# Tridiagonalisation by Householder reflections: pivot and squared norm in a matmul of their own, reflector and update weights on other engines

## The reference, cut to what matters

```python
def _L0_gnn_ref(features, A, W1, b1, W2, b2):
    deg = jnp.sum(A, axis=0) + jnp.sum(A, axis=1) - jnp.diagonal(A)
    d_inv_sqrt = jnp.where(deg > 0, jax.lax.rsqrt(deg), 0.0)
    L_norm = d_inv_sqrt[:, None] * (jnp.diag(deg) - A) * d_inv_sqrt[None, :]
    _, U = jnp.linalg.eigh(L_norm)
    agg = jnp.einsum('mn,bnd->bmd', U.T, features)
    out = jax.nn.relu(agg @ W1 + b1) @ W2 + b2
    return jnp.einsum('nm,bmd->bnd', U, out)
```

## Time and profile before

| what | value |
|---|---|
| device time, median of 3 runs | 1482.2 us (1481.74 to 1482.93) |
| profiled execution: device time | 1483.62 us |
| profiled execution: span from first to last instruction | 1481.8 us |
| 127 reflections (L297 first to last) | 14.5 to 386.5 us |
| eigenvalues and vectors | about 390 to 665 us |
| layers | about 666 us to the end |
| mean granted TensorE clock | 0.888 of full speed |

### The profile page before, as it was taken

How to read it: one execution, slowest core, us unless ns; L and a number is a source line. 1 busy time by engine, 2 the same in 40 slices (tenths; PEclk the granted TensorE clock), 3 DMA queues, 4 the chain that set the end, 5 groups by cost and what they waited for, 6 DMA issues and landing times.

```text
span 1481.8 us, 24437 instructions
## 1 busy us (share of the span) xinstructions
PE 1024.0 (69%) x6001; PEld 834.4 (56%) x6001; DVE 1125.8 (76%) x5634; ACT 793.1 (54%) x2905; POOL 172.3 (12%) x464
## 2 busy tenths in 40 slices
PE   5777777777640000008998889988799978899875
PEld 4666666666430000005796666976668956679754
DVE  6888888888799889983457784566865678845677
ACT  3555555555320000004777866777767778677786
POOL 2111111111200000001011010111020120201111
PEclk9999999999975555558999899999899999999987
DMA  0000000000200000001000010000010000100000
GB/s 2 1 1 1 1 1 1 1 1 1 56 20 1 1 1 1 1 0 57 1 2 1 1 39 22 1 1 1 8 53 1 1 1 2 30 0 1 1 1 29
DMA packets 19903, 12.94 MB, mean 9 GB/s; under 512 B 1153, under 2 KB 18722, under 8 KB 19746
## 3 DMA queue, kind: packets, MB, share of 16 engines
q1 hardware_dynamic: 19746, 11.23, 2.8%
HBM read 7.03 MB, written 4.19 MB: 8 GB/s over the span
## 4 chain that ended last, share of the span: by engine, by line
PE 32%; DVE 11%; ACT 8%; issue 2%; POOL 1%; DMA 0%; DVEq 0%; POOLq 0%; ACTq 0%
PE P L1036 11%; PE P L981 6%; PE P L1044 6%; ACT x L1138 2%; PE P L986 2%; ACT S L1209 2%; DVE stats L1248 2%; PE P L1098 1%; DVE S L1320 1%; DVE top L1325 1%; DVE t L1338 1%; PE P L1053 1%; PE P L1082 1%; POOL t L969 1%; ACT t L1189 1%
## 5 line engine op out<-in xcount | busy, mean ns | idle before, releaser
L461 PE MATMUL sumP<-ident_tail,Yb 128*128 128x128 f32 x1 | 0.5, 473 | 215.6 <-DVE Yb L623 215.6
L193 PE MATMUL productP<-M,ident_tail 128*128 128x127 f32 (+63 forms) x254 | 87.3, 441 | 71.3 <-DVE M L313 71.3
L1036 PE MATMUL P<-t,WihT 128*128 128x128 f32 (+1 forms) x832 | 119.4, 290 | 10.9 <-POOL t L969 10.9
L1044 PE MATMUL P<-step_h,WhhT 128*128 128x128 f32 (+2 forms) x768 | 123.4, 304 | 0.0
L490 ACT ACTIVATE small<-small 128x1 f32<-128x1 f32 x1 | 0.2, 203 | 229.1 <-DVE small L596 229.1
L461 PEld LDWEIGHTS sumP<-ident_tail,Yb 128*128 128x128 f32 x1 | 0.2, 183 | 215.7 <-DVE Yb L623 215.7
L1036 PEld LDWEIGHTS P<-t,WihT 128*128 128x128 f32 x832 | 109.9, 191 | 14.4 <-POOL t L969 13.7
L193 PEld LDWEIGHTS productP<-M,ident_tail 128*128 128x128 f32 x254 | 63.6, 311 | 95.1 <-DVE M L313 95.1
L1161 ACT ACTIVATE gate_i<-P,half_bias 128x128 f32<-128x128 f32 (+3 forms) x160 | 69.1, 432 | 89.3 <-PE P L1044 65.3
L962 POOL TENSOR_TENSOR rstd<-variance,minus_half 128x4 f32<-128x4 f32 x64 | 64.5, 1007 | 442.4 <-DVE variance L1258 442.4
L1044 PEld LDWEIGHTS P<-step_h,WhhT 128*128 128x128 f32 x768 | 108.9, 191 | 4.5 <-DVE step_h L1291 0.7
(11 more groups left out here) (322 smaller groups left out, 3159.6 us busy)
## 6 DMA issues: line engine op xcount, KB each, us to landing
xin<-x SPq DMA_DIRECT2D x16, 256.0 KB, 2.8
out<-y SPq DMA_DIRECT2D x16, 256.0 KB, 2.3
W<-L_gnn_W SPq DMA_DIRECT2D x3, 64.0 KB
Wqkv<-L_gnn_W SPq DMA_DIRECT2D x1, 192.0 KB
Wg<-L_gnn_Wg SPq DMA_DIRECT2D x2, 64.0 KB
A<-adj SPq DMA_DIRECT2D x1, 64.0 KB, 2.0
b<-L_gnn_b SPq DMA_DIRECT2D x1, 64.0 KB
bg<-L_gnn_bg SPq DMA_DIRECT2D x1, 64.0 KB
```

Of the source, the lines that this page charges most:

```text
L193: pe.matmul(productP[:, remaining], tails, M[:, remaining], start=True, stop=True).then_inc(product_ready, 1)
L1036: last = pe.matmul(place, c["WihT"][:, p - 1, gate * H:(gate + 1) * H], sources(s, p, t), start=bank not in fresh, stop=not t, skip_group_ ...
L1044: last = pe.matmul(gate_place(s, p, t, gate), c["WhhT"][:, p - 1, gate * H:(gate + 1) * H], step_h[s][:, 0:G * windows(p)], start=False, s ...
```

## The change

The row product is split in two. TensorE first makes two columns alone, the pivot and the squared norm (into the new PSUM tile `pivotP`), then the row. ScalarE copies the two columns, takes the root, and copies the row when it comes; VectorE takes pivot and squared norm from the two-column copy. `v_col` is made on ScalarE and written straight into `reflectors`; beta goes straight into `E` and the gain straight into `gains`, with their signs turned once at the end of the loop (`E` on VectorE, `gains` on GpSimd in the next block). The weights of the second half of the update are put together from products that ScalarE (`SPREAD_V`, `GAINED_M`, `INNER_V`, `REST`) and GpSimd (`INNER`) make; of them VectorE keeps `SPREAD`, `PART` and `NU`. Per reflection VectorE has 15 arithmetic instructions in place of 17, ScalarE 10 in place of 8, GpSimd 3 in place of 2, TensorE 5 matmuls in place of 4.

```diff
@@ GpSimd, each reflection @@
                 pool.wait_ge(inverses_ready, now)
                 pool.sem_inc(inverses_seen, 1)
+                pool.wait_ge(beta_ready, now)
+                nc.gpsimd.tensor_tensor(col(INNER), inverses[:, 0:1], E[:, k:k + 1], ALU.mult).then_inc(inner_ready, 1)
                 nc.gpsimd.tensor_tensor(open_gain[:], inverses[:, 1:2], below[:, now:now + 1],
@@ TensorE @@
-                pe.matmul(tailP[:, now:N + 1], tails, ident_tail[:, now:N + 1], start=True, stop=True).then_inc(tail_row_ready, 1)
+                pe.matmul(pivotP[:, 0:2], tails, ident_tail[:, now:N + 1:N - now], start=True, stop=True).then_inc(pivot_ready, 1)
+                pe.matmul(tailP[:, remaining], tails, ident[:, remaining], start=True, stop=True).then_inc(tail_row_ready, 1)
@@ ScalarE @@
-                act.wait_ge(tail_row_ready, now)
-                nc.scalar.activation(row_square[parity][:, now:N + 1], tailP[:, now:N + 1], ACT.Copy).then_inc(row_copied, 1)
-                nc.scalar.activation(norm, tailP[:, N:N + 1], ACT.Sqrt, bias=tiny[:]).then_inc(norm_ready, 1)
+                act.wait_ge(pivot_ready, now)
+                nc.scalar.activation(pivots[parity][:], pivotP[:, 0:2], ACT.Copy).then_inc(pivot_copied, 1)
+                nc.scalar.activation(norm, pivotP[:, 1:2], ACT.Sqrt, bias=tiny[:]).then_inc(norm_ready, 1)
+                act.wait_ge(tail_row_ready, now)
+                nc.scalar.activation(rows[parity][:, remaining], tailP[:, remaining], ACT.Copy).then_inc(row_copied, 1)
                 act.wait_ge(beta_ready, now)
+                nc.scalar.activation(v_col, ident[:, now:now + 1], ACT.Identity, bias=tail, scale=beta).then_inc(v_ready, 1)
                 act.wait_ge(matrix_ready, now)
...
+                nc.scalar.activation(col(BETA_M), M[:, now:now + 1], ACT.Copy, scale=beta).then_inc(beta_m_ready, 1)
                 act.wait_ge(v_ready, now)
                 act.wait_ge(gain_ready, now)
...
+                nc.scalar.activation(col(NGV), v_col, ACT.Copy, scale=gain).then_inc(scaled_ready, 1)
+                act.wait_ge(spread_ready, now)
+                nc.scalar.activation(col(SPREAD_V), v_col, ACT.Copy, scale=col(SPREAD)).then_inc(spread_v_ready, 1)
+                act.wait_ge(beta_m_ready, now)
+                nc.scalar.activation(col(GAINED_M), col(BETA_M), ACT.Copy, scale=gain).then_inc(gained_m_ready, 1)
+                act.wait_ge(spread_v_ready, now)
+                act.wait_ge(inner_ready, now)
+                nc.scalar.activation(col(INNER_V), col(SPREAD_V), ACT.Copy, scale=col(INNER)).then_inc(inner_v_ready, 1)
+                act.wait_ge(gained_m_ready, now)
+                act.wait_ge(coef_ready, now)
+                nc.scalar.activation(col(REST), col(SPREAD_V), ACT.Identity, bias=col(GAINED_M),
+                                     scale=col(COEF)).then_inc(rest_ready, 1)
@@ VectorE @@
+                v.wait_ge(pivot_copied, now)
...
...
+                v.wait_ge(inverses_ready, now)
+                V.scalar_tensor_tensor(gain, inverses[:, 0:1], -1.0, norm, ALU.mult, ALU.mult).then_inc(gain_ready, 1)
+                V.tensor_tensor(col(SPREAD), inverses[:, 0:1], square, ALU.mult).then_inc(spread_ready, 1)
+                v.wait_ge(row_copied, now)
+                v.wait_ge(beta_ready, now)
+                whole_row = t.done(V.tensor_tensor(first, first, beta, ALU.add))
...
...
+                v.wait_ge(rest_ready, now)
+                part = t.done(V.scalar_tensor_tensor(col(PART), product_colP[:, 0:1], gain, col(REST), ALU.mult, ALU.add))
...
-                t.step(V.scalar_tensor_tensor(col(NU), col(NGV_NORM), col(G), col(NGP), ALU.mult, ALU.add))
+                v.wait_ge(inner_v_ready, now)
+                t.until(part)
+                t.step(V.scalar_tensor_tensor(col(NU), p_rowP[:, now:now + 1], col(INNER_V), col(PART), ALU.mult, ALU.add))
...
@@ VectorE, once, behind the loop @@
...
+            V.tensor_tensor(scrap[:], M[:], ident, ALU.mult).then_inc(diag_ready, 1)
...
@@ GpSimd, once, at the start of spectral_vectors @@
-            nc.gpsimd.tensor_tensor(T[:], ident, gains[:], ALU.mult).then_inc(gains_turned, 1)
+            t.step(nc.gpsimd.tensor_tensor(T[:], ident, gains[:], ALU.mult))
+            nc.gpsimd.tensor_scalar(T[:], T[:], -1.0, None, ALU.mult).then_inc(gains_turned, 1)
```

More of the change, by code:

```diff
@@ L62, in spectral_basis @@
     small = sb("small", [N, 32])
-    row_square = [sb(f"row_square_{j}", [N, N + 1]) for j in range(2)]
-    v_col = sb("v_col", [N, 1])
+    rows = [sb(f"row_{j}", [N, N]) for j in range(2)]
+    pivots = [sb(f"pivot_square_{j}", [N, 2]) for j in range(2)]
     tiny = sb("tiny", [N, 1])
@@ L115, in col @@
         return small[:, j:j + n]
-    (ABS, BETA, NTAU, NKB, COEF, Q, G, BETA_M, NGV, NGV_NORM, NGP, NU, DEGREE, DEG, DI, SOME, EXPONENT, DIAG, ROWSUM,
-     TABLE) = range(20)
+    (ABS, SPREAD, INNER, COEF, Q, BETA_M, GAINED_M, NGV, SPREAD_V, INNER_V, REST, PART, NU, DEGREE, DEG, DI, SOME, EXPONENT,
+     DIAG, ROWSUM, TABLE) = range(21)
     def every_reflection(reflect):
@@ L218, in reflect @@
                 act.wait_ge(beta_ready, now)
+                beta, v_col, gain = E[:, k:k + 1], reflectors[:, k:k + 1], gains[:, k:k + 1]
+                nc.scalar.activation(v_col, ident[:, now:now + 1], ACT.Identity, bias=tail, scale=beta).then_inc(v_ready, 1)
                 act.wait_ge(matrix_ready, now)
-                nc.scalar.activation(col(BETA_M), M[:, now:now + 1], ACT.Copy, scale=col(BETA)).then_inc(beta_m_ready, 1)
-                nc.scalar.activation(E[:, k:k + 1], col(BETA), ACT.Copy, scale=-1.0).then_inc(edges_ready, 1)
+                nc.scalar.activation(col(BETA_M), M[:, now:now + 1], ACT.Copy, scale=beta).then_inc(beta_m_ready, 1)
@@ L265, in reflect @@
                 after = k + 2
[L266 to L271, removed]
+                pivot, square = pivots[parity][:, 0:1], pivots[parity][:, 1:2]
+                first, v_row = rows[parity][:, now:now + 1], rows[parity][:, remaining]
+                sign, beta, gain = signs[:, k:k + 1], E[:, k:k + 1], gains[:, k:k + 1]
                 norm = divisors[parity][:, 1:2]
-                t.done(V.scalar_tensor_tensor(col(ABS), first, -1.0, first, ALU.mult, ALU.max))
-                prepared = t.done(V.tensor_scalar(sign, first, 0.0, 2.0, ALU.is_ge, ALU.mult))
+                v.wait_ge(pivot_copied, now)
+                t.done(V.scalar_tensor_tensor(col(ABS), pivot, -1.0, pivot, ALU.mult, ALU.max))
+                prepared = t.done(V.tensor_scalar(sign, pivot, 0.0, 2.0, ALU.is_ge, ALU.mult))
                 v.wait_ge(norm_ready, now)
@@ L284, in reflect @@
[L284 to L285 removed]
+                whole_row = t.done(V.tensor_tensor(first, first, beta, ALU.add))
                 v.wait_ge(product_ready, now)
                 t.until(whole_row)
[L290 to L291 removed]
+                V.tensor_tensor_reduce(out=scrap[:, remaining], in0=productP[:, remaining], in1=v_row, scale=inverses[:, 0:1],
+                                       scalar=0.0, op0=ALU.mult, op1=ALU.add, accum_out=col(COEF)).then_inc(coef_ready, 1)
@@ L297, in reflect @@
+                t.wait()
                 V.scalar_tensor_tensor(tail, open_tail[:], col(COEF), col(Q), ALU.mult, ALU.subtract).then_inc(tail_ready, 1)
[L300 to L303, removed]
+                v.wait_ge(rest_ready, now)
@@ L310, in reflect @@
-                v.wait_ge(scaled_norm_ready, now)
-                t.until(parts)
-                t.step(V.scalar_tensor_tensor(col(NU), col(NGV_NORM), col(G), col(NGP), ALU.mult, ALU.add))
+                half = t.done(V.scalar_tensor_tensor(M[:, remaining], p_rowP[:, remaining], col(NGV), M[:, remaining], ALU.mult,
+                                                     ALU.add))
+                v.wait_ge(inner_v_ready, now)
+                t.until(part)
+                t.step(V.scalar_tensor_tensor(col(NU), p_rowP[:, now:now + 1], col(INNER_V), col(PART), ALU.mult, ALU.add))
```

38 lines of the change are left out of this document (21 added, 17 removed).

## The result

The changed kernel takes 1499.03 us (median of 4 runs, 1497.21 to 1506.25) beside 1482.57 us for the kernel before on the same chip (4 runs, 1481.74 to 1483.76). The ratio is estimated from all the runs as 1.0118, with a 95% interval of 1.0091 to 1.0145 (the quotient of the two medians is 1.0111): slower by about 16.5 us. The forecast was 1510.5, in a range of 1490 to 1525. The direction and the place are as forecast; the size is a good half of the 28.3 us that the terms add up to.

A forecast was written before the change was run, and what follows sets the result against it. VectorE's own instruction order was taken to bound the loop; the change would make PART wait for ScalarE's REST. 27.9 - 0.2 - 0.2 + 0.8 = 28.3 us on 1482.2 gave 1510.5 us, range 1490 to 1525.

The forecast's parts named there:

- VectorE's own order: Loop of 127 reflections: VectorE's instruction order and result latencies make the 2.89 us period; other engines fit beneath.
- the shortcut: Two-column pivot copy: ready 1.10 us after the tail, but VectorE is at the update until 1.35, so no gain.
- REST at the end of ScalarE's queue: Loop: REST, last of seven activations, lets PART start 1.88 us after beta; period 3.11, 0.22 more.
- VectorE's list: Loop, from beta to the tail: 1.21 to 1.31 us, taken as 1.28, 0.2 later than before.
- 5 x 0.20: ScalarE's queue: five activations with a scale column hold it 0.20 us each, so REST starts 1.47 after beta.
- its own signs: Wrong if activations start closer than 0.2 us, VectorE isn't idle ahead of PART, or pivot work waits for its copy.
- The seams: Around the loop: mending E beside the matmul saves 0.2 us, the first reflection 0.2; T's sign costs 0.8.
- the sign of T: Block behind the loop: GpSimd turns it ahead of its tables while VectorE waits, costing 0.8 us.
- the first (the shortcut decides): Loop: with REST at +1.61 or earlier, 0.05 to 0.12 us a period is saved, 1472 us; chance 0.06.
- The second (a second column operand free): ScalarE's queue: v_col and REST save 0.08 us each, loss 0.06 a period, 1490 us; chance 0.05.
- The third, waits inside the queue: ScalarE: one dependent distance of 0.33 instead of 0.20 adds 0.13 a period, 1527 us; 0.07 with GpSimd's rival.
- The fourth, GpSimd late: Loop: open_gain later by 0.5 us delays Q and the tail, 29 us more, 1540; 0.07 with the queue-wait rival.

The follow-up runs named there:

- the last experiment: The changed kernel with ScalarE's and VectorE's instructions reordered, v_col made on VectorE, and REST's sum split into two VectorE instructions: 1455.01 us, 0.9817 of the kernel before.
- REST earlier: The changed kernel with ScalarE's queue reordered so that REST is sixth of seven, ahead of INNER_V: 1488.29 us, 1.0050 of the kernel before.
- the pivot ahead: The kernel before with only the row split: two-column matmul, copy and root first, the row behind; 1482.90 us, 1.0009 of the kernel before.
- both orders together: The changed kernel with REST ahead of INNER_V, whole_row ahead of the gain, the tail waiting for Q alone, open_gain ahead of INNER: 1481.26 us, 0.9982.
- with v_col on VectorE: The changed kernel with ScalarE's and VectorE's instructions reordered and v_col made on VectorE behind SPREAD: 1476.54 us, 0.9952 of the kernel before.

## Why the prediction was right, and where its size was off

- **VectorE's own order bounds the kernel before; the shortcut gives nothing there.** The second is shown: alone it moved the loop by 0.02 us and the time by 0.09%, inside what can be told from no change. The first is read from the empty waits, and the last experiment bears it out: PART 0.24 us sooner after beta than G, and a period 0.22 shorter, with the rest of the period at 0.77 + 0.46 in both.
- **REST at the end of ScalarE's queue sets the period.** Shown by the wait of PART on L247, and by taking one activation away and adding one.
- **VectorE's list, tail at +1.28.** Measured +1.32. Up to Q the terms were right (+0.96 forecast and measured); the tail stands 0.36 behind Q (224.52 to 224.88) where 0.25 and 0.07 for two more semaphores were taken, just outside the bound of 0.10 for them. It didn't count, since REST was later; in the run with REST earlier it did.
- **What failed: the term "5 x 0.20" for five activations, and its neighbours.** The 0.20 came from L220 and L221 in the earlier trace rows. Here the queued ones follow each other by 0.186: L234 at 224.03 and L247 at 224.97, 0.94 for five. `v_col` holds 0.29 (0.28 taken) and starts at +0.18 (0.19 taken). So REST starts at +1.41 instead of 1.47 and PART at +1.81 instead of 1.88. 0.07 x 127 = 9 us, which is the difference between the 27.9 forecast for the loop and the 18.5 that came. L220 starts after ScalarE's wait for beta, and an activation that does so lasts longer (0.294 before; here 0.386 for `v_col` beside 0.372 for `REST`), so I took the price of the first of a queue for all of it. By its own signs the prediction was wrong here: it named activations closer than 0.2 us, and PART came at +1.81 instead of 1.85 to 1.95, its wait ended by REST in 115 of 127 reflections instead of all. The row that I trusted was one of an activation that had waited. The Trainium skill, page "ScalarE: Activation LUTs", section "What ACT_TABLE_LOAD costs", gives 186 ns and the columns for an activation with immediates, about 93 more per column operand and about 93 of overlap between neighbours; the estimate from it had PART at +1.81 and 19 us more in the loop. The trace agrees with these figures: 0.279 and 0.372 us for the queued ones with one column and with two, 0.186 apart.
- **The seams.** E beside the matmul −0.2 and the sign of T +0.7 came as forecast (−0.2, +0.8). The first reflection, from its tail to the next one, is 0.07 shorter (3.11 to 3.04), not 0.2. The +0.43 between D and T wasn't foreseen. Between these two blocks GpSimd clears the semaphores of the loop, and the change has six more of them. The kernel before with the pivot ahead has two more, and its rows lie between:

```profile
389.02 0.29 DVE L332 COPY D<-tailP 128x128 f32<-128x128 f32 x1 [0.89 <-PE tailP L207]
392.94 0.45 POOL L414 TENSOR_TENSOR T<-ident_tail,gains 128x128 f32<-128x128 f32 x1 [7.08 <-POOLq L1380]
```

From D to T it is 3.78 us with none more, 3.92 with two and 4.20 or 4.21 in all eight kernels with six, 0.07 for each. The three points fit the clearing as the cause; no run changes the number of semaphores alone.

- **The layers.** 2.0 us of the gap to the forecast lie in an unchanged part. Its busy time on TensorE (708.66 and 708.46 us) and its mean clock (0.94) don't show why. Windows of the same work (but for a few instructions at their ends), before and after, tell more. In this stretch the granted clock went from 0.90 to 0.96, and it took 3.2 us less:

```profile
765.90:855.50 89.60, 75.34 (x586) 62.51 (x588) 65.14 (x218) 68.10 (x242) 10.77 (x17) 0.90 0.01 1
785.30:871.70 86.40, 72.40 (x588) 60.66 (x590) 64.95 (x217) 68.19 (x242) 10.45 (x17) 0.96 0.00 1
```

The rest took 1.2 us longer, so the net gain sits where the clock rose; that the clock is the cause is a reading of these rows. The whole part varied from 814.6 to 823.6 us over these kernels. The forecast can't claim these 2.0 us: with the layers as before the loss would have been near 18.5 us.

Of the rivals, the first (the shortcut decides) needed PART at +1.61 or sooner; it fell, with PART at +1.81. REST earlier brought PART to +1.63, and both orders together brought the loop 5.7 us below that of before. The second (a second column operand free) would have had both two-operand activations at one-column length: they last 0.386 and 0.372, not 0.29. The third, waits inside the queue, fell: the five stand 0.186 apart, with no gap although each waits for a semaphore or two. The fourth, GpSimd late, fell too: VectorE waits for nothing of it.

## What to carry to other kernels

When work is taken off a busy engine and given to one that takes its instructions in order, count where the first operand that is needed stands in that queue; while that operand is the last to come, each instruction ahead of it costs about its full spacing on every turn of the loop, however idle the engine is on average. Take the spacing from rows of instructions that start right behind another, not from those that start after a wait. And before an operand is made earlier, look in the timeline at what its reader does until then: here the shortcut for the pivot was worth nothing, because its reader was busy until later.

## What the runs showed of the hardware

- A 128x1 activation that had to wait for its operand lasts about 14 ns longer than one that starts 0.186 us behind another (0.386 against 0.372 us with two column operands; 0.294 before the change against 0.279 with one). It is enough that it starts 0.02 us late: with v_col on VectorE, REST starts 0.21 behind the activation ahead (206.63 to 206.84), which is still running, and lasts 0.386.
- In the change the tail starts 0.36 us after Q (224.52 to 224.88), behind two waits for other engines and two for VectorE's own results. Where the last one is folded into Q's step, and `open_gain` is made earlier, it starts 0.25 after it (198.20 to 198.45 in the last experiment). The instruction lasts 0.22 in both. Which of the two edits gives the 0.11 wasn't run apart.
- The same 4869 matmuls, of the layers but for five, were busy for 703.5 us at a mean granted clock of 0.95 and for 714.9 at 0.93, in executions of kernels that differ only before them.
- The code between two blocks grew with the number of semaphores that it clears: 3.78 us from D to T, 3.92 with two more, 4.20 or 4.21 with six more.
